# Second attention and last feed-forward in one block: the gates, the norm, the transpositions and the products dealt out over the attention units

## What is computed

```python
def _gates(cls_tok, Wr):
    logits = cls_tok @ Wr.T
    top_vals, top_idx = jax.lax.top_k(logits, K)          # K = 2 of E = 8
    ... masked softmax over the two
gates = _gates(x[:, 0, :], Wr)                             # from row 0 of each batch alone
mid = jnp.einsum('blh,erh->belr', x, A)                    # R = 64
expert_out = jnp.einsum('belr,ehr->belh', mid, Bw)
weighted = jnp.einsum('be,belh->blh', gates, expert_out)
return x + weighted                                        # x here is the normalised x

x = x + _L1_xattn_ref(_layernorm(x), ctx_1024, ctx_1024, ...)
x = x + _L1_ffn_ref(_layernorm(x), Wr, A, Bw)
```

## Time and profile before

| | |
|---|---|
| median of 3 runs | 547.41 us (544.65 to 548.41) |
| the profiled execution | 543.16 us |
| its span, first to last instruction | 541.4 us |
| PE busy | 487.1 us (90%) |
| DVE, ACT, POOL busy | 294.2, 190.7, 214.9 us |
| mean granted clock of TensorE | 0.956 |
| second attention's first scores | 412.86 us after the start |
| last block's first PE instruction | 514.64 us |

### The profile page before, as it was taken

How to read it: one execution, slowest core, us unless ns; L and a number is a source line. 1 busy time by engine, 2 the same in 40 slices (tenths; PEclk the granted TensorE clock), 3 DMA queues, 4 the chain that set the end, 5 groups by cost and what they waited for, 6 DMA issues and landing times. The chain is left out here.

```text
span 541.4 us, 9559 instructions
## 1 busy us (share of the span) xinstructions
PE 487.1 (90%) x3126; PEld 394.0 (73%) x3126; DVE 294.2 (54%) x671; ACT 190.7 (35%) x426; POOL 214.9 (40%) x291
## 2 busy tenths in 40 slices
PE   4799998579999999988999999999856999997587
PEld 3577775256787778767999999999734777675475
DVE  4588877363054122223555455545445688986493
ACT  2445544076450012002333323332212644543053
POOL 3210140144241557424995543333334635410075
PEclk9999999769999999989999999999957999999799
DMA  8998100020000222899513332221175000000013
GB/s 305 395 403 237 2 1 1 11 79 0 2 1 10 93 73 103 262 347 312 95 41 100 97 99 80 70 70 60 40 231 168 1 2 0 2 1 1 0 41 117
DMA packets 48352, 53.52 MB, mean 99 GB/s; under 512 B 14737, under 2 KB 42706, under 8 KB 48050
## 3 DMA queue, kind: packets, MB, share of 16 engines
q1 hardware_dynamic: 33794, 22.49, 14.9%
q0 software_dynamic: 7152, 19.67, 10.7%
q10 hardware_dynamic: 7360, 10.75, 6.3%
HBM read 35.78 MB, written 17.12 MB: 98 GB/s over the span
## 5 line engine op out<-in xcount | busy, mean ns | idle before, releaser
L130 POOL TENSOR_TENSOR rstd<-var,mhalf 128x2 f32<-128x2 f32 x32 | 22.5, 703 | 129.2 <-DVE var L123 129.2
L1133 PE MATMUL banks<-w_hi,xgT_hi 128*128 x156 | 54.8, 352 | 1.4 <-ACT xgT_hi L821 1.4
L426 DVE TENSOR_REDUCE mx<-banks 128x16 f32<-128x1024 f32 x32 | 39.0, 1219 | 30.2 <-PE banks L287 30.0
L1299 DVE TENSOR_TENSOR hgT_lo<-banks,hgT_hi 128x256 fp32r<-128x256 f32 x78 | 24.1, 350 | 56.4 <-ACT hgT_hi L987 56.4
L980 ACT ACTIVATE hg<-banks 128x352 f32<-128x352 f32 x39 | 18.1, 464 | 104.1 <-PE banks L1137 91.8
L1134 PE MATMUL banks<-wd,xgT_hi 128*128 x156 | 50.4, 324 | 0.0
L1070 PE MATMUL banks<-sdn,big 128*128 128x256 f32 x192 | 49.2, 404 | 0.0
L1070 PEld LDWEIGHTS banks<-sdn,big 128*128 128x128 f32 x192 | 34.9, 194 | 13.5 <-issue 9.6
L141 ACT ACTIVATE xn<-x,shift,rstd 128x256 f32<-128x256 f32 (+1 forms) x64 | 34.9, 600 | 27.3 <-POOL shift L132 26.0
L287 PE MATMUL banks<-kvb,qT 64*128 64x256 f32 x256 | 36.3, 402 | 7.6 <-DVE ps L429 3.4
L1057 PE MATMUL banks<-xn2T_hi,sgu_hi 128*128 128x512 f32 (+1 forms) x96 | 38.8, 404 | 0.7 <-DVE xn2T_lo L1191 0.7
(11 more groups left out here) (216 smaller groups left out, 1106.9 us busy)
## 6 DMA issues: line engine op xcount, KB each, us to landing
w_hi<-in_egu POOLq DMA_DIRECT2D x2, 2816.0 KB, 20.7
expert_rows_in<-zeros SPq DMA_DIRECT2D x1, 5304.0 KB, 41.9
xn<-expert_rows_in SPq DMA_DIRECT2D x39, 128.0 KB, 2.0
y_all<-choices_out SPq DMA_DIRECT2D x16, 256.0 KB, 5.0
wd<-in_egu ACTq DMA_DIRECT2D x8, 352.0 KB, 10.3
wd<-in_egu ACTq DMA_DIRECT2D x4, 704.0 KB, 9.4
out_x<-fo SPq DMA_DIRECT2D x8, 256.0 KB, 2.2
x<-in_x ACTq DMA_DIRECT2D x2, 768.0 KB, 9.7
```

The costliest lines, as they stand in the source:

```text
L426: nc.vector.tensor_reduce(mx, heads(psS), AX.X, ALU.max).then_inc(max_done.sem, 1)
L1133: nc.tensor.matmul(to, xgT_hi[:, c, k, :], hi, start=(k == 0), stop=False)
```

## The change

The last block goes. Its work is put into slots of the attention block, whose tables grow to all four engines and to new places in the lists: `x{u}` and `o{u}` (PE, in front of transpose_x and project_o, where they hold only waits), `inverse{u}` and `exps{u}` (ACT), "last output but one" and "end". All slots of one number stand where they stood; ACT's slot 16 is now ahead of inverse(7), and POOL has one.

The gates move forward: row_stats from slot 8 to 6, row_norm from 10 to 7, row_columns from 14 to 8, row_logits from 15 to 9, spread_columns and choose to 9, gates to 11, batch_matrix(0) and (1) to PE's slots 11 and 12. The statistics of the last norm for units 0 to 7 go to DVE's slots 4, 6, 8, 10, 12, 14, "last output but one" and "end". The transpositions (turn3) and products (product3) of units 0 to 7 follow on PE from slot 9 on. PSUM comes from the attention's own banks 4 and 7, and towards the end from the banks of the scores and their transpositions, so each turn3 and product3 waits for what used its bank before. xn and its transpose have a place for each unit now; x + xn and the result are written over x; SP stores each unit from x when its result is there.

```diff
@@ attention
                 wait(pe, qT_ready, u)
+                other_work("tensor", f"x{u}")
...
                 wait(pe, resid_done, u)
+                other_work("tensor", f"o{u}")
...
             project_o(NU - 2)
+            other_work("tensor", "last output but one")
             values(NU - 1)
             other_work("tensor", 2 * NU)
             project_o(NU - 1)
+            other_work("tensor", "end")
...
@@ kernel
+        PSX, PSW, FIRST, SECOND = psum[4], psum[7], psum[0], psum[1]
+        TURNED_IN = [PSX, PSW, PSX, PSX, PSX, psum[2], psum[3], psum[2]]
+        MADE_IN = [PSW, PSW, PSW, FIRST, SECOND, FIRST, SECOND, FIRST]
...
         def row_columns():
             nc.tensor.wait_ge(f_row, 1 + B)
+            wait(nc.tensor, events["resid_done"], 3)
...
+        def weigh_second_factor(b):
             nc.vector.wait_ge(f_gcol, 2 * B)
             nc.vector.wait_ge(ffn1_in, 48)
+            for k in range(KR):
+                v.tensor_scalar(fbg[:, b, k, :], fb[:, k, :], gcol[:, b, k:k + 1], None, ALU.mult).then_inc(f_scaled, 1)
...
         def batch_matrix(b):
             nc.tensor.wait_ge(f_scaled, (b + 1) * KR)
+            if b == 0:
+                wait(nc.tensor, events["qT_ready"], 7)
+            else:
+                nc.tensor.wait_ge(f_g, 1)
+                wait(nc.tensor, events["resid_done"], 5)
...
+        def stats3(u):
+            wait(nc.vector, events["resid_done"], u + 1)
+            ln3.stats(nc.vector, x, u // 2, u % 2)
...
+        def add_norm(u):
+            wait(nc.gpsimd, ln3.xn_ready, UT * u + UT)
+            nc.gpsimd.wait_ge(f_row, 1 + B)
+            rows = unit_rows(u)
+            nc.gpsimd.tensor_tensor(rows, rows, xn3[:, u, :, :], ALU.add).then_inc(f_summed, 1)
...
+        def turn3(u):
+            wait(nc.tensor, ln3.xn_ready, UT * u + UT)
+            if u in (0, 2, 3):
+                wait(nc.tensor, events["qT_ready"], 6 if u == 0 else NU)
+            if u == 1:
+                wait(nc.tensor, events["resid_done"], 4)
+                nc.tensor.wait_ge(f_g, 1)
+            if u == 4:
+                nc.tensor.wait_ge(f_xT, 4)
...
+        def copy3(u):
+            nc.scalar.wait_ge(f_xt, u + 1)
+            nc.scalar.activation(xT3[:, u, :, :], TURNED_IN[u].rearrange("p (k n) -> p k n", k=KD), ACT.Copy).then_inc(f_xT, 1)
...
+        def product3(u):
+            nc.tensor.wait_ge(f_xT, u + 1)
+            nc.tensor.wait_ge(f_wb, B)
+            if u in (0, 1, 2):
+                wait(nc.tensor, events["resid_done"], (5, 6, 6)[u])
+                wait(nc.tensor, f_added, u)
+            elif u in (3, 4):
+                wait(nc.tensor, events["sub_done"], 2 * NU)
+            else:
+                nc.tensor.wait_ge(f_added, u - 1)
...
+        def add3(u):
+            nc.vector.wait_ge(f_y, u + 1)
+            nc.vector.wait_ge(f_summed, u + 1)
...
+        tensor_work = {8: row_columns, 9: lambda: (row_logits(), turn3(0)), 10: lambda: turn3(1), 11: lambda: batch_matrix(0),
+                       12: lambda: batch_matrix(1), 13: lambda: (turn3(2), product3(0)), 14: lambda: product3(1),
+                       15: lambda: (turn3(3), product3(2)),
+                       "last output but one": lambda: turn3(4),
+                       16: lambda: (product3(3), turn3(5), product3(4)),
+                       "end": lambda: (product3(5), turn3(6), product3(6), turn3(7), product3(7)),
+                       "x6": lambda: nc.tensor.wait_ge(f_xT, 1), "x7": lambda: nc.tensor.wait_ge(f_wb, 1),
+                       "o3": lambda: nc.tensor.wait_ge(f_g, 1), "o4": lambda: nc.tensor.wait_ge(f_xT, 2),
+                       "o5": lambda: nc.tensor.wait_ge(f_added, 1), "o6": lambda: nc.tensor.wait_ge(f_added, 3)}
+        scalar_work = {7: lambda: normalise3(0), "exps4": lambda: copy3(0), 9: lambda: normalise3(1),
+                       "inverse5": lambda: (copy3(1), gate_exp()), 11: lambda: (normalise3(2), keep_matrix(0)),
+                       "inverse6": lambda: keep_matrix(1), "exps6": lambda: copy3(2), 13: lambda: normalise3(3),
+                       "exps7": lambda: (copy3(3), normalise3(4)), 16: lambda: normalise3(5),
+                       "end": lambda: (copy3(4), copy3(5), normalise3(6), copy3(6), normalise3(7), copy3(7))}
+        vector_work = {4: lambda: stats3(0), 6: lambda: (row_stats(), stats3(1)), 7: row_norm, 8: lambda: stats3(2),
+                       9: lambda: (spread_columns(), choose()), 10: lambda: stats3(3),
+                       11: lambda: (gates(), weigh_second_factor(0), weigh_second_factor(1)), 12: lambda: stats3(4),
+                       13: lambda: add3(0), 14: lambda: stats3(5), 15: lambda: (add3(1), add3(2)),
+                       "last output but one": lambda: stats3(6), 16: lambda: (add3(3), add3(4)),
+                       "end": lambda: (stats3(7), add3(5), add3(6), add3(7))}
+        gpsimd_work = {6: row_rstd, 7: lambda: (rstd3(0), rstd3(1)), 9: lambda: rstd3(2), 11: lambda: (rstd3(3), add_norm(0)),
+                       13: lambda: (rstd3(4), add_norm(1), add_norm(2)),
+                       15: lambda: (rstd3(5), add_norm(3), add_norm(4)),
+                       16: lambda: (rstd3(6), add_norm(5), rstd3(7), add_norm(6), add_norm(7))}
...
-        with nc.Block() as block:
...
-                batch_matrix(1)
-                front(0, 0)
-                front(0, 1)
-                pe.wait_ge(f_wb, B)
...
-                over_pairs(pe, NU // 2 - 1, pair)
...
```

More of the change, by code:

```diff
@@ L405, in _ @@
                     inverse(u - 1)
+                other_work("scalar", f"inverse{u}")
                 if u + 1 < NU:
@@ L409, in _ @@
                 exps(u, 0, 1)
+                other_work("scalar", f"exps{u}")
                 if u + 2 < NU:
@@ L480, in _ @@
             residual(NU - 2)
+            other_work("vector", "last output but one")
             weigh(NU - 1)
@@ L484, in _ @@
             wait(dve, resid_done, NU)
+            other_work("vector", "end")
         @block.gpsimd
@@ L1350, in xattn_ffn_kernel @@
                              "f_wb", "f_sum"))
+        f_xt, f_xT, f_y, f_added, f_summed, f_store = (
+            sem(n) for n in ("f_xt", "f_xT", "f_y", "f_added", "f_summed", "f_store"))
+        mem3 = {"stats": space("stats3", 2 * UT * 6).rearrange("p (b t n) -> p b t n", b=2, t=UT), "mhalf": mem["mhalf"]}
+        for name in ("mv", "var", "rstd", "nmean", "shift"):
+            n = 2 if name == "mv" else 1
+            flat = space(name + "3", 2 * UT * n)
+            mem3[name] = flat.rearrange("p (b t n) -> p b t n", b=2, t=UT) if n == 2 else flat.rearrange("p (b t) -> p b t", b=2)
+        ln3 = LayerNorm(nc, ctx, "ln3", mem3)
+        out_t = out.rearrange("(t p) n -> p t n", p=P)
         v = nc.vector
         links = 0
+        PSX, PSW, FIRST, SECOND = psum[4], psum[7], psum[0], psum[1]
+        TURNED_IN = [PSX, PSW, PSX, PSX, PSX, psum[2], psum[3], psum[2]]
+        MADE_IN = [PSW, PSW, PSW, FIRST, SECOND, FIRST, SECOND, FIRST]
         def link(ins):
@@ L1401, in row_logits @@
                 for k in range(KD):
-                    last = nc.tensor.matmul(psum[4][:, 64 + b * E:64 + (b + 1) * E], xcol[:, b, k, :], wr[:, k, :],
+                    last = nc.tensor.matmul(PSW[:, 64 + b * E:64 + (b + 1) * E], xcol[:, b, k, :], wr[:, k, :],
                                             start=(k == 0), stop=(k == KD - 1))
@@ new lines, in normalise3 @@
+        def normalise3(u):
+            ln3.normalise(nc.scalar, x, u // 2, u % 2, out=xn3[:, u, :, :])
+        def add_norm(u):
[12 more added lines that the diff above has]
+                nc.tensor.wait_ge(f_xT, 4)
+            if u in (5, 6):
+                wait(nc.tensor, events["exp_done"], 4 * NU)
+            if u == 7:
+                nc.tensor.wait_ge(f_xT, 6)
+            for t in range(UT):
+                for k in range(KD):
+                    last = nc.tensor.transpose(TURNED_IN[u][:, k * UN + t * P:k * UN + (t + 1) * P],
+                                               xn3[:, u, t, k * P:(k + 1) * P], mem["ident"][:, :])
+            last.then_inc(f_xt, 1)
@@ new lines, in copy3 @@
+        def copy3(u):
[11 more added lines that the diff above has]
+                nc.tensor.wait_ge(f_added, u - 1)
+            for t in range(UT):
+                for k in range(KD):
+                    last = nc.tensor.matmul(MADE_IN[u][:, t * D:(t + 1) * D], xT3[:, u, k, t * P:(t + 1) * P],
+                                            wb[:, u % 2, k, :], start=(k == 0), stop=(k == KD - 1))
+            last.then_inc(f_y, 1)
@@ new lines, in add3, with store @@
+        def add3(u):
+            nc.vector.wait_ge(f_y, u + 1)
+            nc.vector.wait_ge(f_summed, u + 1)
+            rows = unit_rows(u)
+            v.tensor_tensor(rows, MADE_IN[u].rearrange("p (t n) -> p t n", t=UT), rows, ALU.add).then_inc(f_added, 1)
+        def store(sp):
+            for u in range(NU):
+                t = tile0(u // 2, u % 2)
```

(3 more changed lines are left out.)

131 lines of the change are left out of this document (21 added, 110 removed).

## The result

The changed kernel takes 554.3 us in the median of four runs (552.25 to 555.5), the kernel before beside it 546.03 (541.13 to 548.41). The ratio is 1.015, with a 95% interval of 1.011 to 1.019.

A forecast was written before the change was run, and what follows sets the result against it. PE was taken to set the pace, with 14.7 us of old idle time and low clock to gain. New waits of 19.2 plus 4.0 of clock made 23.2, so 8.5 longer: 547.41 + 8.5 = 555.9 us, range 548.5 to 562.

The forecast's parts named there:

- Rivals 1 and 2: Rival 1: waits come, clock falls at most once, +1.0 to +5, chance 0.24; rival 2: faster, -9.1 us, chance 0.06.
- the third one: Rival 3, much slower: clock falls after each of four waits, POOL's additions block DVE; +12 to +15.5 us, chance 0.12.
- The sign that would have made the prediction wrong: PE waiting less than 12 us in slots 9, 11 and 15 together.
- (a): stats3(0) in DVE's slot 4: its small operations meet POOL's L494 addition and are blocked; 1.2 us, bounds 0 and 1.2.
- (b): row_stats and stats3(1) in slot 6: PE waits 2.5 us in unit 3, up to 0.7 more beside POOL's bias additions.
- (c): Slot 9: row_logits on PE waits for spread_columns behind weigh(3); 2.95 us, taken as 4.1 with stats3(2) meeting L494.
- (d): Slot 11: batch_matrix(0) on PE waits for gates and the first four scalings; 5.5 us, bounds 5.0 and 6.9.
- (e): Slot 15: product3(2) on PE waits for add3(1) to free its bank, transpose_s(7,1) queued behind; 4.0 us.
- (f): The end, behind project_o(7): copies between turns and products of units 6 and 7 make PE wait; 1.4 us, bounds 0.7 and 2.
- (g): Small gaps of PE in the steady units, 0.5 us as before.
- (h): Low granted clock behind PE's waits: 2.6 us after slot 11 plus one fall of 1.4, 4.0 in all; bounds 0 and 8.
- The end of the block: Eight stores from the same queue as before, only earlier: 0 us; the barrier between the blocks counted as going.

The follow-up runs named there:

- product2_late: Changed kernel with product3(2) and its addition moved from slot 15 to slot 16, after values(7); 554.23 us, ratio 1.0128 to the kernel before.
- fillers: Changed kernel with 21 products of constants, results unread, put into PE's waits in slots 7, 9, 11 and 15; 548.39 us, ratio 1.0039 to the kernel before.
- spread8: Changed kernel with spread_columns moved from DVE's slot 9 to slot 8, between the two shifts; 549.39 us, ratio 1.0063 to the kernel before.
- reordered_matrix11: The reordered one with batch_matrix(0) put back from slot 12 to slot 11; 548.19 us, ratio 0.9954 to the kernel before.
- before_filler: The kernel before with 13 products of constants on PE in its long wait ahead of batch_matrix(0); 547.55 us, ratio 0.9963 to the kernel before.
- reordered_nodrain: The reordered one without the drain of POOL at the end of its attention blocks; 538.21 us, ratio 0.9774 to the kernel before.
- reordered2: reordered_nodrain with row_rstd ahead of POOL's additions, weigh_second_factor(1) in DVE's slot 12, copy3(2) in ACT's 14; 538.25 us, ratio 0.9785 to the kernel before.
- reordered3: reordered2 with normalise3(0) moved to ACT's slot 8 and normalise3(4) to slot 16; 540.21 us, ratio 0.9787 to the kernel before.
- the reordered one: Changed kernel's functions in other places: spreading in slot 8, matrices in 12 and 13, turns and products rearranged; 535.06 us, ratio 0.9805 to the kernel before.

## Why the prediction was right, and where a term was not

The forecast of 555.9 us (+8.5) stands against 554.3 (8.3 more than beside it). That the two agree so closely is in part luck: the two profiled executions, from which the terms are read, differ by 11.0 us, and the errors of the terms cancel. Rivals 1 and 2 fell; of the third one half came true, the clock that falls four times. The sign that would have made the prediction wrong, less than 12 us in slots 9, 11 and 15 together, was close: they are 12.2 us. Step by step:

- **(a) the statistics of slot 4:** taken 1.2, measured 0. The two tensor_scalars start at 439.09 and 439.18, POOL's addition at 439.19. They were ahead by a hundredth of a microsecond, as the low bound had it. That such a meeting holds DVE up was right (1149 and 156 ns in two kernels, and 1153 ns again for row_stats in slot 6, which (b) had counted); that it happens here was not. The last of the two and the addition:

```profile
439.18 0.16 DVE L123 TENSOR_SCALAR var<-mv 128x2 f32<-128x2 f32 x1
439.19 2.62 POOL L503 TENSOR_TENSOR x<-x,y_all 128x512 f32<-128x512 f32 x2
```

- **(b) slot 6:** taken 2.5, measured 2.54.
- **(c) slot 9:** taken 4.1, measured 2.63. Without the meeting that I had carried over from (a) I had 2.95; most of the other 0.3 is that stats3(2) did not make DVE late, which sat idle for 0.80 us before the maximum.
- **(d) slot 11:** taken 5.5, measured 5.70. Here POOL and DVE did meet: two operations of the gates take 0.69 and 0.65 us where 0.17 is usual, beside POOL's bias additions at 485.60:

```profile
485.67 0.69 DVE L1456 TENSOR_TENSOR gt_gate<-gt_hot,gc_e 128x16 f32<-128x16 f32 x1
486.39 0.65 DVE L1457 TENSOR_TENSOR gt_gate<-gt_gate,gt_hot 128x16 f32<-128x16 f32 x1
```

- **(e) slot 15:** taken 4.0, measured 3.87. What I wrote was queued behind it, transpose_s(7,1), does wait; product2_late showed that project_o(6) would have waited too.
- **(f) the end:** taken 1.4, measured 0.69 twice.
- **(g) small gaps:** taken 0.5, measured 0.2. The waits sum to 16.3 us where I had 19.2.
- **(h) the clock** is the term that was mis-sized: taken 4.0 us for two falls, measured 7.0 (fillers), for falls after all four waits. Behind a single wait the size varies by over 1 us from trace to trace (product2_late). I had taken one fall among the waits of 2.5, 4.1 and 4.0 us, since a wait of 1.30 had had none; already 2.54 and 2.63 us of it were enough in this trace. In the kernel before it was 2.45 where I had 2.6.
- **The end of the block** I had at 0, "stores from the same queue". It is 0.9 us, and POOL's drain, which ends 1.1 us behind SP, accounts for it. I had counted the barrier between the blocks as won, 1.28 us of PE's idle time in the kernel before; most of it was paid for there.

Within the stretch, then, 4.2 us are idle time and 5.0 more busy time, of which the low clock is 4.5, where the forecast had 7.1 and 1.4. The mechanism was the one forecast, new waits of PE for DVE and a low clock behind them, but its weights were not: (a), (c) and (g) were 3.0 us too large together, (h) was 3.0 too small and the drain 0.9, and that left the sum near (8.5 forecast, 9.2 in the stretch). What is shown by what: the waits in slots 6, 11 and 15 and at the end are shown by row, the clock by fillers, slots 9 and 11 by spread8 and reordered_matrix11. That scores(2,0) also started 0.9 us later I put down to neither kernel. scores(0,0) starts between 412.9 and 415.4 us in six of the eleven traces, and between 417.2 and 420.5 in the five of before_filler, reordered_matrix11, reordered_nodrain, reordered2 and reordered3; beside these five the kernel before too took 550.6 to 550.9 us, against 546.0 to 546.8 beside the others. The ratios take that out. Why it varies no run shows.

## What to carry to other kernels

When work of one engine is dealt out into the list of another stage, count for each piece the time from the last instruction that both its own engine and its supplier depend on, along both lists, and give it the first place at which the supplier is there; PE reached slots 9, 11 and 15 after 3.9, 3.9 and 2.6 us, and DVE had their inputs ready after 6.5, 9.6 and 6.3. Count PSUM banks as suppliers too. A wait of PE costs more than its length when the clock falls behind it (3.7 us for one of 2.6, 7.9 for 5.6 more, each from one pair of traces): with one long wait cut into four, idle time rose from 12.1 to 16.3 us, but the clock's cost from 2.45 to 7.0. And the same functions in better places made the kernel 2% faster than the kernel before instead of 1.5% slower.

## What the runs showed of the hardware that I had not expected

- The drain of POOL at the end of a block took 7.7 us in the changed kernel, 8.9 in the reordered one, and 1.4 in the small last block of the kernel before. In that last one it was hidden; in the other two it ended 1.1 and 1.8 us behind SP. What sets its length no run shows.
- The granted clock fell to its lower level behind waits of PE of 2.54 and 2.63 us, and stayed at 1.00 behind 1.30, 1.28 and 1.32 us. It is not the length alone: in product2_late the scores behind the same 2.54 us take 1.13 us, at full clock. The Trainium skill (TensorE: Matmul & The Clock Gate, "HAM oscillation — how this bites in real kernels") has bursts parted by waits start cold; the four falls agree, the full clock in product2_late does not.
- A DVE operation on two numbers took 1149 ns beside an addition of POOL and 156 ns without it. The same collision did not happen in slot 4, where DVE was 0.01 us ahead. The Trainium skill (SBUF — State Buffer, "SBUF: two separate sides") describes an exclusive lock between GpSimd and some operations of VectorE, held for a whole instruction by whichever starts first; the pair of numbers agrees with it, and that this very operation is one of those no run here shows.
